# Loop bodies of four sequences in place of two, on every engine and in every stage

## The reference

```python
x = x + _layernorm(_L0_attn_ref(_layernorm(x), W_qkv, W_out))     # linear attention, 16 heads of 8, causal
x = x + _layernorm(_L0_ffn_ref(_layernorm(x), centroids, ...))    # 16 experts, the 2 best per token, 2 shared
x = x + _layernorm(_L1_attn_ref(_layernorm(x), gamma, beta, ...)) # softmax attention, 16 heads of 64, rope
x = x + _layernorm(_L1_ffn_ref(_layernorm(x), w1, w2, h1, h2, w3))# gated, two hidden layers of 512
```

## Time and profile before

| | |
|---|---|
| three runs | 1240.1, 1242.49, 1244.9 us; median 1242.49 |
| the profiled execution's own time | 1241.68 us |
| its span | 1239.9 us, 32,078 instructions |
| busy | PE 92%, DVE 79%, ACT 62%, POOL 46% |
| instruction fetches | queues q8 and q14: 76 packets, 0.97 MB |

### The profile page before, as it was taken

The page is one execution under the profiler, slowest core; times in us unless marked ns, Lnnn a source line. Parts: engine busy times, 40 slices in busy tenths (PEclk is TensorE's granted clock), DMA queues, the critical chain, the costliest instruction groups (busy, mean ns, idle before and its releaser), DMA issues.

```text
span 1239.9 us, 32078 instructions
## 1 busy us (share of the span) xinstructions
PE 1142.7 (92%) x10554; PEld 937.9 (76%) x10554; DVE 979.5 (79%) x2499; ACT 768.2 (62%) x2314; POOL 570.4 (46%) x729
## 2 busy tenths in 40 slices
PE   3888887899999699999999999999999987999997
PEld 2556665899999567777777777777777766999996
DVE  6688887688888576887788787788887776788885
ACT  2555553232222199898889898889988894434432
POOL 2677775555555644454445444545544442111112
PEclk9999999899999799999999999999999999999999
DMA  8000000000000000000000000000000000000000
GB/s 281 18 2 0 0 1 2 1 1 1 0 0 1 1 1 2 2 2 1 2 2 0 0 0 0 0 0 0 0 0 1 1 1 2 8 10 13 9 12 19
DMA packets 14304, 12.32 MB, mean 10 GB/s; under 512 B 1779, under 2 KB 12565, under 8 KB 13973
## 3 DMA queue, kind: packets, MB, share of 16 engines
q1 hardware_dynamic: 14228, 11.34, 3.0%
HBM read 9.24 MB, written 2.10 MB: 9 GB/s over the span
## 4 chain that ended last, share of the span: by engine, by line
PE 72%; DVE 11%; issue 7%; POOL 5%; ACT 2%; DVEq 1%; POOLq 0%; ACTq 0%
PE bank L191 23%; PE bank L977 10%; PE bank L1042 10%; PE bank L1071 10%; PE bank L1084 5%; PE bank L840 4%; PE bank L1258 2%; POOL rstd L365 2%; DVE la_work L507 2%; DVE stat L298 2%; PE bank L560 1%; PE bank L552 1%; PE bank L795 1%; PE bank L383 1%; DVE mv L303 1%
## 5 line engine op out<-in xcount | busy, mean ns | idle before, releaser
L994 ACT ACTIVATE work<-bank,work 128x256 f32<-128x256 f32 x512 | 235.6, 473 | 59.9 <-DVE work L986 59.2
L986 DVE TENSOR_REDUCE work<-bank 128x2 f32<-128x512 f32 x256 | 164.0, 682 | 113.2 <-PE bank L977 113.2
L1008 POOL TENSOR_TENSOR work<-work 128x512 f32<-128x512 f32 x64 | 66.6, 1040 | 279.2 <-DVE work L1002 279.2
L960 POOL TENSOR_TENSOR work<-work 128x512 f32<-128x512 f32 x128 | 164.2, 1283 | 29.6 <-DVE work L952 15.6
L1014 ACT ACTIVATE work<-work 128x256 f32<-128x256 f32 x384 | 161.6, 509 | 0.0
L1042 PE MATMUL bank<-ident,work 128*128 128x128 f32 x1024 | 141.4, 278 | 4.9 <-DVE work L950 1.5
L1042 PEld LDWEIGHTS bank<-ident,work 128*128 128x128 f32 x1024 | 111.2, 141 | 38.2 <-issue 20.2
L1071 PE MATMUL bank<-work 128*64 128x256 f32 x1024 | 138.5, 392 | 0.5 <-DVE work L1057 0.5
L840 PE MATMUL bank<-WrT,moe_work 128*128 128x128 f32 x1024 | 137.9, 279 | 0.0
L977 PE MATMUL bank<-work 32*128 32x256 f32 x2048 | 130.4, 391 | 2.5 <-ACT work L994 1.6
L363 POOL TENSOR_SCALAR ve<-mv 128x2 f32<-128x2 f32 x128 | 28.8, 225 | 221.4 <-DVE mv L303 221.3
(11 more groups left out here) (176 smaller groups left out, 2868.3 us busy)
## 6 DMA issues: line engine op xcount, KB each, us to landing
X<-in_x SPq DMA_DIRECT2D x4, 512.0 KB, 6.0
wF<-in_L_ffn_h_w SPq DMA_DIRECT2D x2, 1024.0 KB, 9.8
out<-X SPq DMA_DIRECT2D x16, 128.0 KB, 1.8
w_qkv<-in_L_attn_w_qkv SPq DMA_DIRECT2D x1, 1536.0 KB, 9.1
WrT<-in_L_ffn_Wr SPq DMA_DIRECT2D x1, 1024.0 KB, 5.0
w_out<-in_L_attn_w_out SPq DMA_DIRECT2D x1, 512.0 KB, 10.4
wF<-in_L_ffn_w_w SPq DMA_DIRECT2D x2, 256.0 KB, 8.4
rope_sin<-in_rope_sin SPq DMA_DIRECT2D x1, 256.0 KB, 3.0
```

Of the source, the lines that this page charges most:

```text
L960: nc.gpsimd.tensor_tensor((QT if kind == "q" else KT)[:, p, a, :], rc[:, ru % 2, :], rs_[:, ru % 2, :], ALU.add).then_inc(c_rope, 1)
L986: nc.vector.tensor_reduce(nmax[:, QUAD * a + j, :], SB_[j][:, :].rearrange("p (t k) -> p t k", t=T), AX.X, ALU.max, negate=True).then_inc( ...
L994: ins = nc.scalar.activation(pr[:, a % 2, j, t, :], SB_[j][:, t * LEN:(t + 1) * LEN], ACT.Exp, bias=nmax[:, h, t:t + 1], accum_out=psum_[: ...
```

## The change

```diff
+        BODY = 4
+
         def over_sequences(eng, step, peeled=2):
-            for i in range(peeled):
+            first = BODY if peeled > 2 else 2
+            rounds = (SEQS - first - 2) // BODY
+            for i in range(first):
                 step(i, i % 2)
-            with eng.Fori(peeled // 2, SEQS // 2 - 1) as j:
-                for p in range(2):
-                    step(eng.snap(j * 2 + p), p)
-            step(SEQS - 2, 0)
-            step(SEQS - 1, 1)
+            with eng.Fori(0, rounds) as j:
+                for q in range(BODY):
+                    step(eng.snap(j * BODY + (first + q)), q % 2)
+            for i in range(first + rounds * BODY, SEQS):
+                step(i, i % 2)
```

## The result

The changed kernel takes 1251.41 us, the median of 6 runs (1250.79 to 1253.2), against 1242.12 us of 6 runs of the kernel before on the same chip (1240.1 to 1244.9): a ratio of 1.0079, with a 95% interval of 1.0068 to 1.009. It is 0.8% slower, where 1243 (1238 to 1247.5) was forecast. Its profiled execution took 1252.52 us with a span of 1250.6, 10.7 more than before (1239.9).

A forecast was written before the change was run, and what follows sets the result against it. PE was taken to set the pace, busy in 92% of the span. 1241.68 us less 3.06 of gains, plus 4.06 for PE's fetch stall and 0.4 for the clock, gave 1243.1, forecast as 1243 us; range 1238 to 1247.5.

The forecast's parts named there:

- item 7: All loops but softmax attention's: bodies stay under one seen kept; DVE's expert body, some 340 instructions, close to ACT's 330.
- The rival with chance 0.11: Expert stage: DVE's doubled body is not kept, its two jumps back stall; 1248.3 to 1251.2, say 1250 us; chance 0.11.
- less what DVE has in hand: Expert stage: DVE's slack of 1.5 us a step, taken off each jump's stall of up to 4.06 us.
- Item 1: Linear attention: three loop edges saved, 1.08 us, and two steps with constant indices, 0.16; gain 1.24 us.
- Item 2: Experts: an edge costs 0.17 us, engines no longer jump together; gain between 0.17 and 0.51, taken as 0.3 us.
- Item 3: Softmax attention: three edges saved, 0.90 us, and two steps from 37.56 to 37.37, 0.38; gain 1.28 us.
- Item 4: Last stage: three loop edges saved at 0.08 us each; gain 0.24 us.
- Item 5: Softmax attention: PE's doubled body, some 3,050 instructions, is not kept; its one jump back stalls, cost 4.06 us.
- Item 6: Softmax attention: ACT's and DVE's doubled bodies may miss, hidden behind PE's stall; cost 0, about 2 us without that cover.
- Item 8: Softmax attention: a 4 us PE pause could lower the clock, worth 0 or 1.7 us; entered at 0.4.
- the pause at L1258: Behind the jump over the Else branch: pause of over 2 us left the clock at 1.00; grounds for entering 0.4 us.
- The row near 1025 us: Profile near 1025 us: PE busy 3.63 of 6 us, granted clock averages 0.72, 3.4 us at the lower level.

## Why the prediction was wrong

The step that failed is item 7, "All other bodies stay under one that is seen to be kept", with its comparison of DVE's expert body (some 340 instructions; in fact 326) to ACT's 330. The sizes were nearly right and the inference was not, since the count of instructions doesn't decide it. 326 instructions on four blocks are fetched again, the same 326 on three are kept, and ACT's 329, kept on three, are fetched again when pushed onto four. With DVE's body kept and all else as forecast, the kernel takes 1243.67 us, and 1243 was forecast. The sign that I had named for this case, long branches of DVE in the expert stage, could not appear: DVE's refetch leaves its branch at 67 ns. The price of the two refetches on PE is the steps 6 to 7 and 10 to 11, 15.22 and 15.59 us in place of 11.69 and 11.49: 3.5 and 4.1, together 7.6. Against the steps with the body kept it is 8.7 over ten steps. Moving the body takes 7.7 us off the median.

The rival with chance 0.11 is what happened, at 1251.4 instead of its 1250, and for about its reason. Its term "less what DVE has in hand" (1.5 us a step) was offset by what it left out, 3.4 us of lower clock behind each pause, worth at most 1.7 us. That the two nearly cancel is luck.

- Item 1, linear attention: 1.24 forecast; 1.6 measured over the looped steps, and 1.5 to 1.65 in four other kernels. Right in kind, somewhat small: steps without an edge take 10.59 us and not 10.67. L467 has 0.43 us of issue in front of it at 117.14, and none of that size in the steps of the earlier trace rows.
- Item 2, experts: the gain forecast at 0.3 us is buried under the pauses. Where the body is kept it is 0.7 (114.1 to 113.4 us over ten steps). In the kernel with DVE at two steps there was no gain but a loss of 1.1.
- Item 3, attention: steps 12 and 13 take 37.35 and 37.39 us, and steps where an edge was now take 37.56. That makes 1.2 of the 1.28. Right.
- Item 4: 0.24 forecast in the last stage. Its starts drew 0.3 closer up to the last step but one. The last step was 0.7 shorter besides, but that is no edge: PE's jump over the Else branch took 3,613 ns in place of 4,271.
- Item 5: right in place and mechanism. PE's body of some 3,050 instructions is refetched at its one jump. The branch took 3,338 ns and not 4,271, and the step 3.1 us more and not 4.06. In other kernels it was 3,317 to 3,998 ns. That PE keeps or drops a body by its blocks, as DVE and ACT do, is argued: no run moved this body.
- Item 6: right. ACT's and DVE's refetches in the attention hide behind PE's, and without that cover DVE's showed 1.26 us, below the "about 2".
- Item 8, the clock: entered at 0.4, with 1.7 as its dear end; the step behind PE's pause took 1.55 more (39.11 in place of 37.56). The clock's own share of it is smaller: at clock 1.00 the same step took 1.20 more, 0.64 of it in PE's break among the scores, which the forecast put at nothing. With 6.8 us at the lower level, in the kernel with DVE's experts at two, it took 3.6 more. The row that I leaned on, the pause at L1258, was the wrong neighbour: nearly nothing runs behind it. The row near 1025 us was the nearer one.

Summed from the measured parts: −1.6 (linear attention), −1.2 (attention: three edges and two steps written out), +8.0 (ten looped expert steps, pauses and gains together), +3.1 and +1.55 (PE's jump and the step behind it) and −0.9 (last stage) make +8.9, against 9.3 between the medians (8.4 to 11.2 by the interval of the ratio). Of the 10.7 between the spans, most of the other 1.8 lie in stretches of lower clock ahead of and in the first attention step, which I don't hold to belong to the change.

The Trainium skill (page "Runtime: NRT & Kernel Launch", section on instruction fetch mechanics) gives the engines other than PE room for 512 instructions, in blocks of 256, and has a taken branch stall when its target lies outside a window of two blocks. By the size of that room DVE's 326 would fit. The runs differ: packets of 8 KB, blocks of 128 by the count, and three of them safe. The same section says that there is no instruction cache to profit from. The traces contradict this and the window: a loop of 1,524 instructions on PE, at least six of its blocks, runs without a single fetch. It also prefers full unrolling, and with this the unrolled kernel at 0.992 agrees.

What stays open: where between 1,524 and some 3,050 instructions PE stops keeping a body, whether a fourth block ever stays, and why stretches of lower clock of 0.8 to 1.5 us at stage changes come in some executions and not in others. That three blocks are kept and four not rests on two bodies, each put on three and on four, ACT's on four in two ways. Why a pause of PE at that jump is followed by 3.4 us at the lower clock in most kernels, by 6.8 in one and by none in another is open too.

## What to carry to other kernels

A loop body is kept or refetched by the number of code blocks that it touches on its own engine, so count them engine by engine, with the body's position, and not from the largest body that another engine keeps. If the program can be written out, write it out: fetching straight code cost nothing here, each jump 0.1 to 0.4 us, and each jump to missing code 3 to 4 us on the engine that sets the pace. When an engine seems to wait for something that was long done, right behind a loop edge, look at the gap between its branch and its next sequencer instruction, and at the queues that bring code.

## What the hardware showed that I had not expected

- A refetch on DVE leaves no long branch: 67 ns for the branch, 2,803 ns until the next register step. On PE the branch itself shows it, 3,338 ns.
- 64 added instructions made a kernel 7.7 us faster (1251.41 to 1243.67), 32 did not (1254.76).
- Behind a jump to code that isn't there, a border of two blocks costs a second time if it lies close: 2.85 and 2.96 us of issue between the third and the fourth of PE's last 16 loads or matmuls, 1.98 and 1.71 on DVE six instructions behind the jump, 0.64 on PE after 30 scores.
- A pause of PE of 3.4 us was followed by 3.5 us at a granted clock of 0.52 (32 matmuls in 3.86 us in place of 2.01), but a pause of the same length in another kernel by none, and the step behind it was longer by 1.55 and by 1.20 us.
- With DVE jumping every two expert steps and PE every four, a step took 11.52 us, with both jumping every two 11.41, and with both every four and the code kept 11.34.
